# First layer of a four-layer image network: tiles prepared ahead of image changes, rows signalled per group, and 25 rounds of products a group in the second block

## What is computed

```python
def _conv_reflect(x, w, bias, dil, pad):
    xp = jnp.pad(x, ((0, 0), (0, 0), (pad, pad), (pad, pad)), mode='reflect')
    out = conv_general_dilated(xp, w, (1, 1), 'VALID', rhs_dilation=(dil, dil))
    return out + bias[None, :, None, None]
def _denoise_block(x, w1, b1, w2, b2, w3, b3, a, b, c):
    trip = _triplets(x)          # each channel with its two neighbours
    xf = trip.reshape(B * T, 3, H, W)
    o = a * _conv_reflect(xf, w1, b1, 1, 2) + b * _conv_reflect(xf, w2, b2, 2, 4) + c * _conv_reflect(xf, w3, b3, 4, 8)
    return jnp.tanh(o).reshape(B, T, H, W)
y = _denoise_block(x, <weights of block 1>)
z = _denoise_block(y, <weights of block 2>)     # x = x + z
```

## Time and profile before

| | us |
|---|---|
| median of 3 runs | 5379.86 |
| lowest and highest | 5368.85, 5382.81 |
| span of the profiled execution | 5383.9 |
| layer 0, first block of products | 74 to 1741 |
| layer 0, second block | 1741 to 3245 |
| layers 1 to 3 | 3245 to 5384 |

### The profile page before, as it was taken

The page is one execution under the profiler, slowest core; times in us unless marked ns, Lnnn a source line. Parts: engine busy times, 40 slices in busy tenths (PEclk is TensorE's granted clock), DMA queues, the critical chain, the costliest instruction groups (busy, mean ns, idle before and its releaser), DMA issues. The chain is left out here.

```text
span 5383.9 us, 178367 instructions
## 1 busy us (share of the span) xinstructions
PE 4994.9 (93%) x78653; PEld 3092.8 (57%) x78653; DVE 3365.2 (63%) x6195; ACT 2396.6 (45%) x2999; POOL 1362.4 (25%) x1629
## 2 busy tenths in 40 slices
PE   4998999899899999999999997998777799999998
PEld 2444444444447569997666663443556466666665
DVE  5543444344342555555555546887999788888888
ACT  1222222222221111111111117885999689899997
POOL 0000000000001111111111100000777355555556
PEclk9999999999999999999999998999999999999999
DMA  8677777777666767667667657998688366666664
GB/s 246 217 228 235 224 228 232 223 223 237 222 209 199 226 200 239 207 203 236 203 208 236 205 178 277 321 325 302 256 308 309 129 152 152 150 150 153 151 152 120
DMA packets 366864, 1166.78 MB, mean 217 GB/s; under 512 B 60457, under 2 KB 61096, under 8 KB 287018
## 3 DMA queue, kind: packets, MB, share of 16 engines
q1 hardware_dynamic: 363928, 1152.98, 69.0%
q10 hardware_dynamic: 2162, 2.39, 0.2%
HBM read 683.58 MB, written 453.51 MB: 211 GB/s over the span
## 5 line engine op out<-in xcount | busy, mean ns | idle before, releaser
L679 PE MATMUL c_p<-c_w,wc 128*32 128x512 f16 x55296 | 3027.2, 381 | 91.1 <-DMA c_w<-xs 81.1
L679 PEld LDWEIGHTS c_p<-c_w,wc 128*32 128x32 f16 x55296 | 1896.0, 97 | 1194.4 <-DMA c_w<-xs 76.2
L739 ACT ACTIVATE c_t<-c_p,cbias,cscale 128x512 f32<-128x512 f32 x512 | 397.9, 777 | 2582.6 <-PE c_p L679 2582.6
L591 DVE TENSOR_SCALAR c_y<-c_t 128x512 f16<-128x512 f32 x256 | 109.2, 426 | 855.1 <-ACT c_t L739 854.1
L601 DVE TENSOR_TENSOR a_x<-c_t,a_x 128x512 f32<-128x512 f32 x256 | 221.3, 865 | 666.7 <-ACT c_t L739 658.5
L1699 PE MATMUL f_P<-f_qh,f_wt 64*64 64x512 f16 x4608 | 545.7, 378 | 1.8 <-DVE f_t L1595 1.8
L1699 PE MATMUL f_P<-f_hl,f_wt 64*64 64x512 f16 x4608 | 545.3, 379 | 0.0
L1860 POOL TENSOR_TENSOR f_y<-f_y,f_x 128x512 f32<-128x512 f32 x256 | 330.7, 1292 | 449.3 <-DVE f_hl L1574 443.2
L1595 DVE SCALAR_TENSOR_TENSOR f_t<-f_P,f_kk,f_ci 128x256 f32<-128x256 f32 x1024 | 423.4, 476 | 12.8 <-PE f_P L1699 7.6
L810 POOL COPY c_y<-c_y 128x16 f16<-128x16 f16 x512 | 85.6, 197 | 1360.7 <-DVE c_y L593 1360.7
L1459 POOL TENSOR_TENSOR e_hl<-e_g,e_hl 128x2048 f16<-128x2048 f32 x63 | 257.1, 4081 | 609.3 <-ACT e_hl L1409 609.3
(11 more groups left out here) (263 smaller groups left out, 5887.4 us busy)
## 6 DMA issues: line engine op xcount, KB each, us to landing
c_w<-xs SPq DMA_DIRECT2D x576, 264.0 KB, 5.6
c_w<-ys SPq DMA_DIRECT2D x576, 264.0 KB, 4.0
d_x<-x SPq DMA_DIRECT2D x128, 1024.0 KB, 7.6
x<-d_x SPq DMA_DIRECT2D x128, 1024.0 KB, 5.1
ys<-c_y SPq DMA_DIRECT2D x576, 132.0 KB
xs<-a_hl SPq DMA_DIRECT2D x70, 1056.0 KB, 9.8
a_x<-in_x SPq DMA_DIRECT2D x256, 256.0 KB, 6.8
a_x<-in_x SPq DMA_DIRECT2D x128, 512.0 KB, 5.2
```

The source lines that it names most:

```text
L679: t = p.matmul(pg[32 * j:32 * j + 32, :], wu[:, blk, wl, var, di, :], buf[:, bk, xl * PW + PAD + dx:xl * PW + PAD + dx + NW], start=(di == ...
L739: s.activation(tt_[n % 3][:, :], pp[:, n % 4, :], ACT.Tanh, bias=cbias[:, blk:blk + 1], scale=cscale[:, blk:blk + 1]).then_inc(c_act, 1)
```

## The change

In both blocks:
- `slot` orders the partitions anew: rows -4 to 19 of a band lie in partitions 0 to 95, rows 20 to 23 and -8 to -5 in 96 to 127.
- `load` takes three DMAs a pair in place of two: one of 32 partitions with the DRAM pattern [CP, 32], and two of 16 partitions with a DRAM pattern of 2 by 8. Each is still 8448 bytes a partition.
- `c_ld` is a semaphore a half and group, and PE waits for its group alone.
- Tiles are started every 7 groups in an image from its group 4 (`first_group`), so tiles of the next image are ready earlier. `p0` and `p1_` come one group later than before, after 15 of its rounds. Only units 0 and u % 16 == 2 of the first block load late. `load_x` and the first `load_res` move.

In the second block alone: DVE copies 96 partitions of high rows and 32 of low rows of the next group into `near`, and 64 partitions of low rows into `twice`; ACT copies the same low rows, shifted by three columns, into the other half of `twice`. The four near offsets then take 4 rounds on `near` and 2 on `twice` (and 4 of low weights on high rows), 25 rounds a group in place of 27. POOL makes the weights for them once (`near_weights`), before the loop.

```diff
-        h8, s = ((1, 0), (0, 0), (1, 1), (0, 1))[row // 8 + 1]
-        v8 = row + 8 * h8 - 16 * s
-        return 8 * (2 * v8 + chan % 2) + 4 * s + 2 * h8 + chan // 2
+        place = row + (36, 24, 0, 0, 0, 0, 0, 4)[row // 4 + 2]
+        return 4 * place + 2 * (chan % 2) + chan // 2
...
+        near = [sb(ctx, f"c_n{i}", [128, 4, PW], F16) for i in range(2)]
+        twice = [sb(ctx, f"c_2{i}", [128, 4, PW], F16) for i in range(2)]
...
-            nxt, half = (u + 1) // 2 + 2, u % 2
-            return (nxt, (g + 2) % 4) if nxt < NG and g // 2 == half else (None, None)
+        def first_group(i):
+            image, j = divmod(i - 3, 8)
+            return 64 * image + 4 + 7 * j if i > 2 else -2
+        steps = {first_group(i) + z: (i, z) for i in range(2, NG) for z in range(4) if first_group(i) + z >= 0}
+        loads_x = {first_group(i - 2) + 4 + 2 * c: (i, c) for i in range(4, NG) for c in range(2)}
...
+        def rows_in(e, n):
+            u, g = divmod(n, 4)
+            e.wait_ge(c_ld[u % 2][g], n_win(u))
+            if n >= 2:
+                e.wait_ge(c_pe, n - 1)
+            return win[u % 2][:, 4 * g:4 * g + 4]
...
+                def copies(n):
+                    w = rows_in(v, n)
+                    v.tensor_copy(near[n % 2][0:96], w[0:96, :, 0:PW]).then_inc(c_nh, 1)
+                    v.tensor_copy(near[n % 2][96:128], w[64:96, :, PW:RW]).then_inc(c_nl, 1)
+                    v.tensor_copy(twice[n % 2][0:64], w[0:64, :, PW:RW]).then_inc(c_2a, 1)
...
+                        if doubled(4 * u + g + 1):
+                            copies(4 * u + g + 1)
...
-                    if u == 0:
-                        p.wait_ge(c_l0[g // 2], 128)
-                    elif g == 0:
-                        p.wait_ge(c_ld[half], n_win(u))
+                    p.wait_ge(c_ld[half][g], n_win(u))
...
+                    for di in (4, 0, 1, 7, 8):
+                        for wl, xl in ((0, 0), (0, 1), (1, 0)):
+                            four(wu[:, blk, wl, :, di], rows4, xl * PW + PAD + DX[di], start=(di, wl, xl) == (4, 0, 0))
+                    i, s = stage_of(n - 1)
+                    if s == 0:
+                        p0(i)
+                    if s == 1:
+                        p1_(i)
+                    for di in (2, 3, 5, 6):
+                        four(wu[:, blk, 1, :, di], rows4, PAD + DX[di])
...
+                    p.wait_ge(c_nh, n_copied(n))
+                    p.wait_ge(c_nl, n_copied(n))
+                    for e, di in enumerate((2, 3, 5, 6)):
+                        four(wnear[:, :, e], near[n % 2], PAD + DX[di])
+                    p.wait_ge(c_2a, n_copied(n))
+                    p.wait_ge(c_2b, n_copied(n))
+                    four(wnear[:, :, 4], twice[n % 2], PAD - 2)
+                    t = four(wnear[:, :, 5], twice[n % 2], PAD - 1, stop=True)
...
+                def copies(n):
+                    w = rows_in(s, n)
+                    s.activation(twice[n % 2][64:128, :, PAD - 2:PAD - 1 + NW], w[0:64, :, PW + PAD + 1:PW + PAD + 2 + NW], ACT.Copy).then_inc(c_2b, 1)
...
-                        for h8 in range(2):
-                            e.dma_start(win[half][gp % 2 + 2 * h8:128:4, 4 * g:4 * g + 4].rearrange("p k w -> p (k w)"),
-                                        dram(src, pair(b, gp, 0, 16 * half + 4 * g) + h8 * (8 * VP - RW),
-                                             [[CP, 16], [RW, 2], [1, 4 * RW]])).then_inc(c_ld[half] if u else c_l0[g // 2], 16)
+                        at = pair(b, gp, 0, 16 * half + 4 * g)
+                        for first, count, off, ap in ((0, 32, 0, [[CP, 32]]), (64, 16, RW, [[12 * VP - 2 * RW, 2], [CP, 8]]),
+                                                      (96, 16, 4 * VP + RW, [[4 * VP - 2 * RW, 2], [CP, 8]])):
+                            e.dma_start(win[half][first + gp % 2:first + 2 * count:2, 4 * g:4 * g + 4].rearrange("p k w -> p (k w)"),
+                                        dram(src, at + off, ap + [[1, 4 * RW]])).then_inc(c_ld[half][g], 16)
...
+                e.wait_ge(w_wn, 6)
...
-                    late = u < NU and half == 0
+                    late = u < NU and u % 16 == 2 or u == 0
```

More of the change, by code:

```diff
@@ L296, in layer0 @@
         h = sb(ctx, "a_hl", [128, 8, 2, PW], F16)
-        wc = [sb(ctx, f"wc{i}", [128, 2, 2, 3, 9, 32], F16) for i in range(2)]
+        wall = [sb(ctx, f"wc{i}", [128, 4032], F16) for i in range(2)]
+        wc = [w[:, 0:3456].rearrange("p (a b v d c) -> p a b v d c", a=2, b=2, v=3, d=9) for w in wall]
+        wn = [w[:, 3456:4032].rearrange("p (v e c) -> p v e c", v=3, e=6) for w in wall]
         ast = sb(ctx, "a_st", [128, 8, 6], F32)
@@ L339, in layer0 @@
         a_sd, a_bn, a_p, a_rt, a_g, a_hi, a_lo, a_pad, w_sw = (sem("a_" + n) for n in ("sd", "bn", "p", "rt", "g", "hi", "lo", "pad", "sw"))
-        c_ld = [sem(f"c_ld{i}") for i in range(2)]
-        c_l0 = [sem(f"c_l0{i}") for i in range(2)]
+        c_ld = [[sem(f"c_ld{i}{j}") for j in range(4)] for i in range(2)]
         c_yd = [sem(f"c_yd{i}") for i in range(2)]
@@ L345, in layer0 @@
         c_pe, c_act, c_hi, c_lo, c_pad, c_bn, c_mm, c_ag = (sem("c_" + n) for n in ("pe", "act", "hi", "lo", "pad", "bn", "mm", "ag"))
-        w_c, w_f, w_t, w_sel, w_hi = (sem("w_" + n) for n in ("c", "f", "t", "sel", "hi"))
+        w_c, w_f, w_t, w_sel, w_hi, w_wn = (sem("w_" + n) for n in ("c", "f", "t", "sel", "hi", "wn"))
+        c_nh, c_nl, c_2a, c_2b = (sem("c_" + n) for n in ("nh", "nl", "2a", "2b"))
         w_td = [sem(f"w_td{i}") for i in range(2)]
@@ L379, in n_win, with doubled, n_copied @@
         def n_win(u):
-            return 128 * sum(1 + (place(r)[2] == 0) for r in range(u % 2, u + 1, 2) if r)
+            return 48 * sum(1 + (place(r)[2] == 0) for r in range(u % 2, u + 1, 2))
+        def doubled(n):
+            return 4 * NU <= n < 8 * NU
+        def n_copied(n):
+            return n - 4 * NU + 1
+        def rows_in(e, n):
[4 more added lines that the diff above has]
+            return win[u % 2][:, 4 * g:4 * g + 4]
         def table_of(u):
@@ L673, in products, with four @@
                         p.wait_ge(c_act, n - 3)
[L674 to L682, removed]
+                    def four(weights, source, at, start=False, stop=False):
+                        for j in range(4):
+                            bk = 4 * g + j
+                            var = 0 if (half, bk) == (0, 0) else (2 if (half, bk) == (1, 15) else 1)
+                            t = p.matmul(pg[32 * j:32 * j + 32, :], weights[:, var], source[:, j, at:at + NW],
+                                         start=start, stop=stop, tile_position=(0, 32 * j))
+                        return t
@@ new lines, in products @@
+                    if not doubled(n):
+                        for di in (2, 3, 5, 6):
+                            for xl in range(2):
+                                t = four(wu[:, blk, 0, :, di], rows4, xl * PW + PAD + DX[di], stop=(di, xl) == (6, 1))
+                        t.then_inc(c_pe, 1)
+                        return
+                    wnear = wn[pr % 2]
+                    p.wait_ge(c_nh, n_copied(n))
+                    p.wait_ge(c_nl, n_copied(n))
+                    for e, di in enumerate((2, 3, 5, 6)):
+                        four(wnear[:, :, e], near[n % 2], PAD + DX[di])
@@ L795, in table, with near_weights @@
                                         over(pt[:, 32:40], [[0, 4], [1, 8], [0, 16]]), ALU.mult).then_inc(w_t, 1)
+                def near_weights(blk, to, done):
+                    hi = wc[0][:, blk, 0]
+                    for z, (rows, of, e, d) in enumerate(((slice(0, 96), slice(0, 96), 0, 2), (slice(0, 96), slice(0, 96), 2, 5),
+                                                          (slice(96, 128), slice(64, 96), 0, 2), (slice(96, 128), slice(64, 96), 2, 5),
+                                                          (slice(0, 64), slice(0, 64), 4, 2), (slice(64, 128), slice(0, 64), 4, 5))):
+                        q.tensor_copy(to[rows, :, e:e + 2], hi[of, :, d:d + 2]).then_inc(w_wn, 1)
+                        q.wait_ge(w_wn, done + z + 1)
                 mirror(0)
                 mirror(1)
+                q.wait_ge(w_hi, 6)
+                near_weights(1, wn[0], 0)
                 for u in range(2 * NU):
                     for g in range(4):
-                        i, s = stage_of(u, g)
+                        i, s = stage_of(4 * u + g)
                         if s == 3:
@@ L916, in _ @@
                             store_y(u, g)
-                        if g == 0 and NU <= u + 1 < 2 * NU:
+                        if g == 0 and NU + 2 <= u + 1 < 2 * NU:
                             load_res(u + 1)
-                        if g == 1 and u // 2 + 4 < NG:
-                            load_x(u // 2 + 4, (half,))
+                        if g == 0 and u in (NU - 4, NU - 3):
+                            load_res(u + 4)
+                        if n in loads_x:
```

(1 more changed line is left out.)

38 lines of the change are left out of this document (18 added, 20 removed).

## The result

| | median of the runs, us | span, us | ratio to before |
|---|---|---|---|
| before | 5381.3 | 5383.9 | |
| after | 7375.3 (7366.7 to 7384.3) | 7374.5 | 1.370 (1.368 to 1.373) |

The change costs 37%. Forecast were 7450, in a range of 6950 to 8450.

The account below looks back on a forecast made before the run. Two DMA engines, filled by the count-2 loads, were taken to bound both blocks: 63 us start + 2890 first block + 2160 second + 175 SP waits + 10 last groups = 5298, with 2139 untouched 7437; stated as 7450, range 6950 to 8450.

Parts of the forecast that it names:

- Two engines, by the outermost count: Window loads, both blocks: the two small DMAs with outermost DRAM count 2 run on two engines, 171 kB a group each.
- Rival A: Window loads spread over 16 engines as before, so the change gains as intended: about 5155 us; chance 0.07.
- Among the four of the stores: First block: the loads' two engines lie among the `ys` stores' four, so each carries 282 kB a group, not 206.
- Rival B: First block: the loads' two engines are not among the stores' four, 206 kB a group; about 6660 us; chance 0.06.
- 282 kB at 25 GB/s: First block: each of two engines carries 282 kB a group at 25 GB/s, 11.3 us a group, 2890 us.
- Rival C: Both blocks: the two engines run at 19.1 GB/s, as when all work; about 9000 us; chance 0.09.
- 211 kB, 2160 us, and 175 us of bubbles: Second block: 211 kB a group per engine, 8.44 us, 2160 us; plus 175 (0 to 350) for SP waiting on stores, both blocks.
- Where PE waits: Both blocks: PE's idle time before `c_w` rows is by far the largest, released by DMA, in every group.
- No wait for `v0`: First block, at tiles: PE's 1.40 us wait for the statistics of `v0` disappears (29 tiles, 41 us).
- Copies: Second block: DVE's three take 2.1 us, its sum 5.4 us a group; ACT's takes 1.8 us; DVE's work hidden behind 8.44.
- Rival D: Second block: DVE's copies at half speed, 7.0 us a group, with loads on 16 engines; about 5560 us; chance 0.03.
- Statistics and image changes, 41 + 65 us in rival A: First block, loads on 16 engines: 41 us saved on tile statistics and 65 of the 83 us lost at image changes.

Follow-up runs that it names:

- e1: The changed kernel with the partitions of its two small load DMAs reordered so their outermost count is 8 instead of 2: 5417 us, ratio 1.006.
- e2: The kernel before with only the changed `slot` and the three load DMAs, two with outermost count 2; 27 rounds, no copies: 7431 us, ratio 1.381.
- e8: The changed kernel, loads untouched, with its `ys` stores as four DMAs a group on sixteen engines, issued by ACT: 6839 us, ratio 1.272.
- e6: e1 with the `ys` stores as four DMAs a group on sixteen engines, issued by ACT instead of SP: 5236 us, ratio 0.974.
- e11: e6 with 27 rounds and no copies in the second block: 5351 us, ratio 0.994.
- e10: e7 with three spread load DMAs a pair in place of its two: 5419 us, ratio 1.007.
- e5: e1 with the `ys` stores still two a group on four engines, but issued by ACT one group late instead of SP: 5488 us, ratio 1.021.
- e7: The kernel before with its `ys` stores in four DMAs a group on sixteen engines, issued by ACT, nothing else: 5337 us, ratio 0.992.

## Why the prediction was right

**Total.** 7450 for 7375, +1.0%. The forecast mechanism is the one that the runs show. Of the signs named, layers 1 to 3 (2138 us), the DMA share (0.40 and 0.42), the rate (128 and 142 GB/s) and the bytes came as said. The profile gives no landing time for the window loads, so that sign stays unread.

**Two engines, by the outermost count.** Right, for a source in DRAM as for a destination: e1, e2, and 54 GB/s at a share of 0.14. Rival A, loads on many engines, was one reordering away; but its price was wrong (below).

**Among the four of the stores.** Right, by e8 and by the packets in flight. Rival B falls.

**282 kB at 25 GB/s.** First block 2890 forecast, 2896 measured: 282 x 256 / 2896 = 24.9 GB/s over the whole block. Rival C, 19.1 GB/s, falls. That 25 held so closely is in part luck: it was read from 2112-byte rows written and used for 8448-byte rows read, and the rate isn't one number. In the first block an 8448-byte packet took 338 ns on average when at most 4 were in flight at its start (25 GB/s), and 418 with 14 or more (20 GB/s). The two engines moved some 27 GB/s each where they worked alone, and the mean over the block came out at 25.

**211 kB, 2160 us, and 175 us of bubbles.** 2266 measured, 106 over. SP waits for an `x1` store once a unit, 62 times, as forecast, and for 10 us on average, longer than the 4 us of the sum:

```profile
SPq L922 <- DMA x<-a_x: 641.0, 62, 15.6
```

But the step behind it was wrong in kind. It had the two engines run dry meanwhile. Cut into slices of 1 us, the DMA share is never under 0.125 in the first block (some 900 of 2896 slices lie between 0.125 and 0.19), and in 21 of 2266 slices of the second (some 1050 between). The two are hardly ever dry; SP's gaps pass while they work. What is measured instead is a lower rate, 211 x 256 / 2266 = 23.8 GB/s; 18 of the 106 us lie in the block's first eight groups alone (127 us, for 109 in the later images). Forecast were 5298 us to the end of layer 0, 5236 are measured: the term of 175 stands for nothing in the first block and for 106 us of another kind in the second. Without that term the forecast would have been 7275, 1.4% under, so it came out close for a reason that isn't the one given.

**Where PE waits.** Forecast was a wait for `c_w` rows in every group of both blocks. In the first it comes 170 times for 256 groups. In the second it comes once a unit, under the name of DVE's copy, from the residual rows that stand behind the loads. The copies put DVE into PE's path, and DVE's own list order ties them to the residual; the prediction named the copy's cost but not this queue.

**No wait for `v0`.** Wrong: PE waits 159 us for the first statistics in the first block, 16 times, and 90 us for the second, where the kernel before had 39 in all for `v0`. I read it as DVE coming late, behind its 1787 us of waiting for `ys` stores. Even in e6, without the two-engine loads, 81 us are left, where the prediction's 41 were to go.

**Copies.** DVE 0.69 to 0.70 us each and 2.08 for three, for 0.70 and 2.1. ACT's 1.92 on the page's mean, for 1.8:

```profile
L795 ACT ACTIVATE c<-c_w 64x2052 f16<-64x2052 f16 x256 | 492.3, 1923 | 239.9 <-DMA c_w<-ys 234.2
```

Rival D falls. (Its 3.7 us at half the speed is twice the 1.9 of overlapping copies; twice the 2.1 is 4.2.) The 5.4 us of DVE a group were close: in e6 DVE is busy 1324 of 1383 us, 5.2 a group, and PE doesn't wait for it in the second block.

**25 rounds for 27.** Worth nothing clear under the loads, as forecast (second block 2266 us, and 2273 in e2 with 27), and 111 us where they are cured (e6, e11), which is the 2 x 0.217 x 256.

**Statistics and image changes, 41 + 65 us in rival A.** Here the forecast of the rival failed. It left out what the spread loads cost, a third DMA on SP and more bytes on eight of the engines: 83 us in e10. With that, the schedule's 62 us are more than gone, and with the stores on four engines and on SP the first block ends 135 us behind. As measured, A is 5417, slower than before and not faster. Whoever had cured the count of two and expected 5155 would have been 260 us off.

**Clock.** Granted 0.81 and 0.84 for 0.98 and 1.00, as "under 1.00" said. PE is busy 1841 us in the first block, 7.2 a group against the 11.3 of the two engines, so the loads cover it.

## What to carry to other kernels

Before a DMA's pattern is changed, write down the outermost count of both its sides and add up the bytes for each engine, not for sixteen; the bytes of the fullest engine at 25 GB/s gave this kernel's first block to 0.2%, while the mean share showed the engines 60% free. Where it can be chosen, put the large count outermost: the same rows with 8 and 2 swapped gave 1958 us. When the transfers are then spread, count the issues on the queue that makes them (about 0.65 us each on SP here), since spreading by more DMAs moves the limit to the issuing engine: stores on sixteen engines gained 21 us in the first block when SP issued them, and another 132 when ACT did.

## What the runs showed that I had not expected

- How much an issuing engine is held: in e5 ACT's evictions wait 769 us in the first block behind two stores a group on four engines. SP has no arithmetic of its own that would be late.
- Two cures that are worth 21 us and -81 us alone, in the first block, are worth 153 together.
- Three DMAs for two, at equal bytes and with counts of 32 and 8, cost 83 us in a block of 256 groups, 0.32 us a group, of which the second block of e10 (1493 us, as e7's) shows nothing: there neither `ys` stores nor tiles stand beside them.
